# One norm's statistics, one key rotation and the last rows' gating, each placed in another slot of an attention loop

## The reference, cut to what matters

```
h = _layernorm(x, axis=-1) * (1 + ca) + sa
x = x + ga * _L1_attn_ref(h, L1_attn_Wqkv, L1_attn_Wk_up, L1_attn_Wv_up, L1_attn_Wo)
h = _layernorm(x, axis=-1) * (1 + cb) + sb
x = x + gb * _L1_ffn_ref(h, ...)
```

## Time and profile before

| | us |
|---|---|
| median of 3 runs | 1036.99 (1035.02 to 1038.63) |
| the profiled execution | 1041.08 |
| its span, first to last instruction | 1039.3 |
| PE busy | 979.9 (94%) |
| DVE busy | 702.1 (68%) |
| ACT busy | 564.4 (54%) |
| POOL busy | 435.1 (42%) |
| mean granted clock of PE | 0.988 |

### The profile page before, as it was taken

One profiled execution on the slowest core, in us unless ns is written; L12 is line 12 of the kernel. 1 busy time (PEld: TensorE's weight loads), 2 busy tenths in 40 slices (PEclk: granted clock), 3 DMA queues, 4 the chain that ended last, 5 costly groups with the idle time before them and its releaser, 6 DMA issues.

```text
span 1039.3 us, 25039 instructions
## 1 busy us (share of the span) xinstructions
PE 979.9 (94%) x9714; PEld 744.7 (72%) x9714; DVE 702.1 (68%) x2121; ACT 564.4 (54%) x1450; POOL 435.1 (42%) x391
## 2 busy tenths in 40 slices
PE   5888999999999999999999899999999999999888
PEld 4566897887887755575647668686968696868546
DVE  4888988988989942313133676866686668676864
ACT  3667778778778742212132475656465556554531
POOL 1320240340551711101003566766667566779610
PEclk9998999999999999999999999999999999999989
DMA  9150000000000003700003222322132213212102
GB/s 315 61 193 2 2 0 0 0 0 0 0 2 2 2 1 72 280 1 0 1 1 86 58 52 51 73 53 51 45 80 52 52 43 82 53 38 57 72 2 83
DMA packets 32812, 52.36 MB, mean 50 GB/s; under 512 B 7760, under 2 KB 17744, under 8 KB 31824
## 3 DMA queue, kind: packets, MB, share of 16 engines
q1 hardware_dynamic: 32720, 51.10, 17.9%
HBM read 21.98 MB, written 2.10 MB: 23 GB/s over the span
## 4 chain that ended last, share of the span: by engine, by line
PE 51%; DVE 6%; ACT 2%; issue 1%; POOL 0%; DMA 0%; SPq 0%
PE quad L2101 11%; PE quad L2060 10%; PE quad L1705 8%; PE quad L2118 6%; PE quad L2004 6%; PE quad L2132 4%; PE quad L2196 1%; DVE act_probs L2456 1%; DVE wq_wo L2470 1%; DVE x_pairs L2486 1%; PE quad L2068 1%; PE quad L1591 1%; PE quad L2023 1%; ACT hT L1604 1%; ACT act_probs L2356 0%
## 5 line engine op out<-in xcount | busy, mean ns | idle before, releaser
L2708 POOL TENSOR_TENSOR act_probs<-act_probs,rden 128x512 f32<-128x512 f32 (+3 forms) x128 | 170.4, 1338 | 117.3 <-DVE rden L2475 117.2
L2356 ACT ACTIVATE act_probs<-act_probs,neg_max 128x256 f32<-128x256 f32 (+3 forms) x256 | 140.9, 553 | 89.7 <-DVE neg_max L2456 89.4
L2060 PEld LDWEIGHTS quad<-hT,ug_queries 128*128 128x128 f32 x1024 | 123.3, 193 | 14.2 <-issue 7.7
L2060 PE MATMUL quad<-hT,ug_queries 128*128 128x128 f32 x1024 | 125.3, 276 | 0.8 <-DVE act_probs L1720 0.5
L2456 DVE CUSTOM_DVE_ANT_0 act_probs<-quad,mask 128x256 f32<-128x256 f32 (+3 forms) x256 | 115.0, 485 | 0.3 <-issue 0.3
L1705 PE MATMUL quad<-hT,ug_raw_switch 128*128 128x512 f32 x256 | 113.9, 595 | 0.0
L1720 DVE SCALAR_TENSOR_TENSOR act_probs<-quad,ws_up,silu_keys 128x512 f32<-128x512 f32 x32 | 24.0, 750 | 97.1 <-ACT silu_keys L1715 97.1
L2101 PE MATMUL quad<-silu_keys,ug_raw_switch 128*128 128x256 f32 (+3 forms) x256 | 80.7, 443 | 7.6 <-DVE neg_max L2456 7.4
L1705 PEld LDWEIGHTS quad<-hT,ug_raw_switch 128*128 128x128 f32 x256 | 47.4, 190 | 55.1 <-issue 54.9
L1715 ACT ACTIVATE silu_keys<-quad,ws_gate 128x512 f32<-128x512 f32 x32 | 22.0, 687 | 118.6 <-PE quad L1705 118.6
L2475 DVE RECIPROCAL rden<-den 128x2 f32<-128x2 f32 x128 | 20.4, 159 | 96.0 <-ACT act_probs L2356 95.9
(11 more groups left out here) (330 smaller groups left out, 2293.7 us busy)
## 6 DMA issues: line engine op xcount, KB each, us to landing
rope_swapped<-gate SPq DMA_DIRECT2D x120, 64.0 KB, 2.0
ug_raw_switch<-gate SPq DMA_DIRECT2D x60, 128.0 KB, 2.3
ug_raw_switch<-in_wmod SPq DMA_DIRECT2D x4, 512.0 KB, 7.3
x_pairs<-in_x SPq DMA_DIRECT2D x4, 512.0 KB, 7.9
x_rows<-x_pairs SPq DMA_DIRECT2D x8, 256.0 KB, 5.0
wq_wo<-in_wq_nopeT SPq DMA_DIRECT2D x1, 2048.0 KB, 8.6
wq_wo<-in_wo SPq DMA_DIRECT2D x1, 2048.0 KB, 13.1
ug_queries<-in_switch_w SPq DMA_DIRECT2D x1, 2048.0 KB, 7.8
```

The source lines that it names most:

```text
L2060: mm = nc.tensor.matmul(out[:, P * i:P * i + P], w[:, kt, HP * half + i, :], k.hT[:, kt, b, cols], start=(kt == 0), stop=(kt == KT - 1))
L2356: nc.scalar.activation(tile, tile, ACT.Exp, bias=neg_max[:, r, e:e + 1], scale=-1.0, accum_out=den[:, r, e:e + 1])\
L2708: nc.gpsimd.tensor_tensor(tile, tile, rden[:, t % RING, :].unsqueeze(2).to_broadcast([P, 2, cols]), ALU.mult)\
```

## The change: what it does

1. `norm_at` gets a place of its own for tile 0: that norm's sums move from slot 3 to slot 1 on DVE, its root from slot 4 to slot 2 on POOL. The scaling stays in slot 6.
2. `key_at` takes a delay for each half: half 1 is now 7 slots behind the fill on DVE (slot 29 in place of 26, in each of the three batches) and 8 on POOL and SP (slot 30 in place of 27). Half 0 stays.
3. `gate_out(14)` moves from slot 126 to 125 on DVE, `add_out(14)` from slot 127 to 126 on POOL.
4. The sums of norm `LAST + 1`, with their wait for `add_out(14)`, move from behind `early_logits(2)` in slot 129 to between `early_logits(0)` and `turn(126)` in slot 128.

```diff
-    def key_at(slot, later):
-        return [(b, f) for f in range(2) for _, b, g in due(slot, later + f, "key") if g == f]
+    def key_at(slot, *later):
+        return [(b, f) for f in range(2) for _, b, g in due(slot, later[f], "key") if g == f]
-    def norm_at(slot, p):
+    def norm_at(slot, p, first=None):
         n, at = divmod(slot, NP)
+        p = first if n == 0 and first is not None else p
         return [plan.norms[n]] if at == p and n in plan.norms else []
...
# DVE
                 if t == SLOTS:
                     early_logits(0)
+                    dve.wait_ge(s["added"], NB - 1)
+                    norms.sums(dve, LAST + 1)
                 if LAG <= t:
                     turn(t - LAG)
                 if t == SLOTS:
                     early_logits(1)
                 if t == SLOTS + 1:
                     early_logits(2)
-                    dve.wait_ge(s["added"], NB - 1)
-                    norms.sums(dve, LAST + 1)
...
-                for b, f in key_at(t, 3):
+                for b, f in key_at(t, 3, 7):
                     rotate_key(b, f)
-                for _, n in due(t, 2 if t < SLOTS - NP // 2 else 3, "out"):
+                for _, n in due(t, 2, "out"):
                     gate_out(n)
-                for g in norm_at(t, 3):
+                for g in norm_at(t, 3, 1):
...
# POOL
-                for b, f in key_at(t, 4):
+                for b, f in key_at(t, 4, 8):
                     add_key(b, f)
...
-                for _, n in due(t, 3 if t < SLOTS - NP // 2 else 4, "out"):
+                for _, n in due(t, 3, "out"):
                     add_out(n)
-                for g in norm_at(t, 4):
+                for g in norm_at(t, 4, 2):
                     norms.root(pool, g)
...
# SP
-                for b, f in key_at(t, 4):
+                for b, f in key_at(t, 4, 8):
                     spread_key(b, f)
```

## The result

The changed kernel takes 1030.54 us (median of 6, 1028.30 to 1031.43), the kernel before beside it 1037.01 (median of 6). The ratio is 0.9928, with a 95% interval of 0.9913 to 0.9943: faster by 7.5 us, between 5.9 and 9.0 (the two medians alone differ by 6.5). The prediction was 1031.8 us, in 1028.5 to 1035.8.

A forecast was written before the change was run, and what follows sets the result against it. PE bounds the kernel (51% of the chain), so gains come from its idle time. Part 1 -3.0, part 2 -2.7, parts 3 and 4 +0.5 sum to -5.2 us: 1036.99 becomes 1031.8 us, range 1028.5 to 1035.8.

The forecast's parts named there:

- the cap: Slot 6: DVE's queue, with the norm's scaling, becomes the limit, so 3.0 us gained in place of 3.6.
- The 2.1: Slot 4: of the 2.48 us of sums moved away, some 2.1 us reach PE's scores.
- The clock term: Behind slot 4's wait: 3 us at half clock hold 1.5 us of full-speed work, won if the clock stays up.
- a wait of about 2.3 us: Slot 4: PE's wait shrinks from 4.62 to some 2.3 us, and the clock is expected not to fall.
- The new wait: Slot 30: PE waits 0.3 to 0.6 us for maxima behind the moved rotation, a sign to look for.
- the first rival: Slot 29: POOL holds both multiplications, the rotation stalls as much as in slot 26, part 2 gives 0; chance 0.16.
- it seems to be held: Slot 26: the long 1.96 us multiplication ends 0.56 us after POOL's normalization, so POOL seems to hold it.
- POOL's addition at nothing: Slot 30: POOL's 1.28 us addition moves in front of the normalization where POOL is busiest; costed at nothing.
- the third rival: Slots 29 to 31: POOL's queue delays the maxima, 7.6 us lost over three batches, 1042.1 us in all; chance 0.06.
- Nothing is gained behind it: Behind the loop: PE's transposes at 990.60 were not held by the scaling, so moving the sums wins nothing there.

The follow-up runs named there:

- e1: Only the first norm's sums (slot 1) and root (slot 2) moved, against the kernel before: 1032.99 us, ratio 0.9950.
- e9: The kernel before with four useless 128x512 products in PE's wait of slot 4, against the kernel before: 1035.20 us, ratio 0.9994.
- e2: Only the second key rotation moved to slot 29, against the kernel before: 1035.33 us, ratio 0.9970.
- e3: Only the end changed (tile 14's gating and addition one slot up, last-but-one norm's sums in slot 128), against the kernel before: 1039.15 us, ratio 1.0004.
- e4: Parts 1 and 2 without 3 and 4, against the kernel before: 1031.97 us, ratio 0.9946.
- e7: e5 with half 1 of the keys rotated in slot 28 in place of 29: 1037.82 us, ratio to the kernel before 1.0010.
- e6: Parts 1 and 3, both key rotations in slots 25 and 26 but ahead of the reciprocal, against the kernel before: 1028.53 us, ratio 0.9929.
- e5: Parts 1 to 3 without part 4, against the kernel before: 1030.20 us, ratio 0.9937.
- e10: e5 with two useless 128x512 products in PE's wait behind the loop: 1029.05 us, ratio to the kernel before 0.9927.
- e12: e6 with e10's two useless products behind the loop: 1028.76 us, ratio to the kernel before 0.9922.
- e11: The changed kernel measured again, unaltered, against the kernel before: 1031.99 us, ratio 0.9944.
- e8: e5 with half 1 of the keys rotated in slot 30 in place of 29: 1032.59 us, ratio to the kernel before 0.9956.

## Why the prediction was right, and where a step was wrong

The sum was -5.2 us. The milestones give -5.97 for the loop, and the two medians -6.5 and -5.5.

**Part 1: -3.0 predicted, -3.6 measured** (e1, both at A and at C). The mechanism held: the statistics hid in slot 1, the wait fell from 4.62 to 1.13 us, and the clock did not fall. What failed was the cap. I let "DVE's own queue (the scaling of this norm in slot 6)" take 0.6 of the 3.6 us. DVE's queue cost nothing there. The 2.1 was too small as well. Counted from the start, the scores of slot 4 begin 9.17 - 5.92 = 3.25 us sooner and the next ones 13.42 - 8.67 = 4.75, so removed wait and clock together were worth 4.75 and not 3.6. The move took more than the 2.48 us of the sums out of the stretch, since the rotation of the query in slot 3 shrank too, from 1.54 to 0.67 us. Before, POOL's normalization began 0.05 us ahead of it and it had to stand; after, it began first (rows of before, then of after):

```profile
583.40 1.04 POOL L2708 TENSOR_TENSOR act_probs<-act_probs,rden 128x512 f32<-128x512 f32 x1 [1.61 <-DVE rden L2475]
...
582.19 0.67 DVE L2482 TENSOR_TENSOR gate<-gate,rope_cos 128x512 f32<-128x512 f32 x1
582.58 1.19 POOL L2709 TENSOR_TENSOR act_probs<-act_probs,rden 128x512 f32<-128x512 f32 x1
```

Of the 4.75 us 1.20 come back by the first value product, 0.97 of them at a place I had not looked at: the first scores of the next tile need its rotated query. POOL's addition for it ends at 585.07 + 1.60 = 586.67 and SP issues two transfers, at 586.69 and 587.23. PE starts at 589.63 after 0.78 us that the profile puts down to nothing. By the trace the second transfer landed at 589.54, 0.09 us before. So it is in all ten profiles with part 1: waits of 0.78 to 0.80 us, and PE starts 0.09 us after the landing; in the four without it PE comes 1.2 to 4.4 us after the landing. The code agrees (`score` waits for `rope_swapped` where a half tile begins). So PE waits there for the transfer, although no run moved it.

**The clock term, 1.5 us, was right in size where it arises:** e9 restores the clock alone and the next scores come 1.49 us sooner. What it adds to the kernel's time isn't shown: e9 had 0.94 us left of it at the first value product, and its ratio can't be told from 1. That a wait of about 2.3 us would leave it alone was safe by a margin, since the wait came out at 1.13. Across the profiles the clock fell in slot 4 after all three waits of 4.62 or 4.63 us (before, e2, e3) and after none of 1.24 us or less. The Trainium skill, "TensorE: Matmul & The Clock Gate" (What's actually happening), has a cold clock of 1.2 GHz and a warm one of 2.4; the two levels agree with the granted 0.50 and 1.00 in slot 4.

**Part 2: -2.7 predicted, -3.1 measured in the change, -2.5 and -2.9 in C (e2, and e4 against e1).** The size of a batch, 0.9, came out as 0.92 to 1.10. By the profile's windows PE's idle time from slot 26 to 34 fell from 1.56 to 1.01 us in the first batch; the rest is in the time of products that waited in between. The new wait, which I put at 0.3 to 0.6 us, is 0.88 to 1.01, so that sign did not come true; the rotation took 1.18 + 1.75 = 2.93 us and not 2.6, since in slot 29 POOL holds the first multiplication too. That was the first rival's mechanism; it was there, and it was smaller than the waits that went away. The rival itself, a rotation that stalls as much in the new place, is what e7 shows for slot 28: 1.76 + 1.95 us and a wait of 2.80. So the gain hung on the slot, and on slot 29 having no query rotation, which I had not argued. That POOL is the cause was only supposed ("it seems to be held"). e6 shows it, 0.65 and 0.68 us with POOL at rest. The kernel before also had it ahead of the loop, 0.684 us for the sin multiplication against 1.956 of the six in the loop:

```profile
L2486 DVE TENSOR_TENSOR x_pairs<-x_pairs,rope_sin x6: 1955/1955/1958, 657.3 to 871.2; 128x512 f32<-128x512 f32 x6
L2486 DVE TENSOR_TENSOR wq_wo<-wq_wo,rope_sin x2: 684/684/685, 557.7 to 560.3; 128x512 f32<-128x512 f32 x2
```

The Trainium skill, "GPSIMD Engine Reference" (Specifications), says that the two engines contend when a vector instruction reads two inputs from SBUF; these rows agree.

**POOL's addition at nothing** was right for slot 30: the third rival, which needed a new wait above 2.2 us, showed in no profile with slot 29 or 30 (at most 1.83), and the query rotations' mean fell from 789 to 724 ns. The two changed groups by form, after (count, then busy us, mean ns), which answer to the earlier trace rows; POOL's own addition did not grow:

```profile
L2487 DVE TENSOR_TENSOR x_pairs<-x_pairs,rope_sin 128x512 f32<-128x512 f32 x6 | 11.1, 1856 | 0.0
L2703 POOL TENSOR_TENSOR x_pairs<-x_pairs 128x512 f32<-128x512 f32 x6 | 7.6, 1274 | 0.0
```

**Parts 3 and 4: +0.5 predicted.** The wait of 3.2 us is as I put it (0.82 - 0.4 by my terms, 0.74 - 0.28 by e5), and DVE showed no wait for POOL's addition. The step that failed is "Nothing is gained behind it". I had read PE's transposes at 990.60 as not held, but they stood behind a product of 2.87 us at half clock. At full clock that product takes 1.55, and then the late scaling does hold PE, for 0.82 us in e2. With the sums moved, D is 9.32 us; at full clock without it (e2, e10, e12), 10.19 or 10.20. So the end is worth +0.44 - 0.88 = -0.4 us where the clock is full, and +0.42 where it is half (e3). Either is inside what e3's interval can tell. None of this moved the forecast out of its range: two gains came out larger than their terms, and 0.17 us of them went again between slots 114 and 122.

**The clock behind the loop was left out of the sum,** and rightly so for a median. It was at half in the profile of before and full in that of after, which makes some 2 of the 10.7 us between the two spans: 12.10 - 10.20 = 1.9 by D. It is no merit of the change. After a wait of 2.76 us it fell in the kernel before and not in e2; after 3.21 us it fell in e11 and not in the first profile of the same kernel. What decides it stays open. Two useless products in that wait kept it full in both kernels that had them (e10, e12); two profiles are not enough to call that certain.

## What to carry to other kernels

Find the slot where the engine that is moved to is at rest or waits anyway, not merely a slot some distance off. And look at which of the two engines begins first: here a DVE multiplication that began before POOL's operation took 0.67 us, and one that began behind it took what was left of POOL's operation and 0.55 more. The same rotation one slot earlier, behind a query's, lost 0.7 to 0.9 us a batch where slot 29 won 1.0, and ahead of the reciprocal it won 1.67. Measure an edit between two near milestones inside the loop: A and the Bs agreed within 0.13 us between two profiles of one loop (but for the late swap of e5, worth 1.3), where medians of one kernel moved by 1.4 us. And when a slow product covers a late input, the input has no slack: ask what the wait would be at full clock.

## What was not expected of the hardware

- The hold by POOL is not one price, but it follows one rule in these traces. The same multiplication of 128x512 took 0.68 us alone, 1.18 us on slot 29's first, and 1.75 or 1.96 us elsewhere, and each held one ends 0.55 us after a POOL operation, once after six of them (5.49 us). POOL comes out longer too: its rope addition of 1.27 us took 1.60 to 1.80, its normalization of 1.46 took 1.92.
- A transfer that is late by a quarter of a microsecond (0.22 to 0.27 us in e5, e8 and e10) went with 1.3 to 1.5 us more in B1: the DVE multiplication then began behind a POOL addition and took 1.64 to 1.68 us.
- Behind the loop the granted clock fell in 10 of 14 profiles, after waits of 2.46 to 3.21 us. It stayed full in four, two with useless products in the wait and two after waits of 2.76 and 3.21 us.
